# Routed experts of a two-layer gated attention and mixture-of-experts kernel: gate and up weights become the stationary operand, and the turning of the activations is dropped

## What is computed

```
# layer 0: 32 experts of inner width 128, 8 chosen for each token
h = silu(flat @ wg.T) * (flat @ wu.T)
acc = acc + w[:, None] * (h @ wd.T)
...
# layer 1: 8 experts of inner width 256, 2 chosen for each token
h = silu(xt @ w1[e].T) * (xt @ w3[e].T)
y = y + gate_e[:, None] * (h @ w2[e].T)
```

## Time and profile before

| | |
|---|---|
| device time, three executions | 1091.81, 1091.92, 1095.67 us; median 1091.92 us |
| span of the profiled execution (first to last instruction) | 1088.8 us |
| median less span: what lies around the span | 3.1 us |
| busy share of the span: TensorE, VectorE, ScalarE, GpSimd | 84%, 64%, 41%, 50% |
| granted TensorE clock, mean over the span | 0.924 |
| routed blocks of layer 0 | about 340 to 601 us of the span |
| routed blocks of layer 1 | about 923 to 1064 us of the span |

### The profile page before, as it was taken

One profiled execution on the slowest core, in us unless ns is written; L12 is line 12 of the kernel. 1 busy time (PEld: TensorE's weight loads), 2 busy tenths in 40 slices (PEclk: granted clock), 3 DMA queues, 4 the chain that ended last, 5 costly groups with the idle time before them and its releaser, 6 DMA issues.

```text
span 1088.8 us, 20608 instructions
## 1 busy us (share of the span) xinstructions
PE 911.9 (84%) x5524; PEld 711.6 (65%) x5525; DVE 701.8 (64%) x1978; ACT 441.5 (41%) x1031; POOL 546.5 (50%) x581
## 2 busy tenths in 40 slices
PE   3368888887658999999999907889999997998883
PEld 3367777777546888888888504655656564786672
DVE  5669999997796865555555268675857256443334
ACT  4558888893053444434444202022223223232220
POOL 7246655644005755555552677878600001787641
PEclk9769999998668999999999968979999997999997
DMA  8960000003103776676777874343300020466648
GB/s 247 223 122 2 1 0 0 0 2 108 44 1 87 233 221 209 217 221 208 217 185 130 291 238 133 97 141 101 107 1 20 1 77 19 84 110 136 135 67 246
DMA packets 75225, 127.44 MB, mean 117 GB/s; under 512 B 12480, under 2 KB 52032, under 8 KB 75008
## 3 DMA queue, kind: packets, MB, share of 16 engines
q0 software_dynamic: 21264, 48.02, 19.4%
q1 hardware_dynamic: 32240, 57.47, 17.4%
q10 hardware_dynamic: 21632, 20.85, 5.5%
HBM read 80.62 MB, written 36.77 MB: 108 GB/s over the span
## 4 chain that ended last, share of the span: by engine, by line
PE 54%; DVE 21%; DMA 8%; issue 7%; POOL 6%; ACT 2%; SPq 2%; DVEq 0%; ACTq 0%; POOLq 0%
PE bank L917 17%; PE bank L932 9%; PE bank L1622 5%; POOL yg L1199 4%; DVE ptl L621 4%; PE bank L906 4%; DMA sw<-in_w 4%; PE bank L427 2%; PE bank L1522 2%; DVE nmax L613 2%; PE bank L925 2%; DVE hot_hi L1341 2%; PE bank L1557 2%; PE bank L1681 2%; PE bank L1582 2%
## 5 line engine op out<-in xcount | busy, mean ns | idle before, releaser
L1182 POOL DMA_INDIRECT xg<-token_rows,gather_idx x198 | 191.7, 968 | 209.1 <-PE bank L906 86.4
L917 PE MATMUL bank<-sw,xgt 128*128 x948 | 244.9, 381 | 0.4 <-issue 0.4
L917 PEld LDWEIGHTS bank<-sw,xgt 128*128 128x128 f32 x948 | 165.4, 191 | 15.5 <-issue 0.8
L1199 POOL DMA_INDIRECT yg<-slot_rows,slot_of x128 | 142.1, 1110 | 59.9 <-issue 34.7
L1011 ACT ACTIVATE ssil<-bank 128x128 f32<-128x128 f32 x237 | 65.8, 278 | 210.8 <-PE bank L917 210.8
L932 PE MATMUL bank<-sw,sht 128*128 x474 | 145.2, 389 | 0.1
L1103 DVE COPY xgt<-bank 128x256 f32<-128x256 f32 x198 | 83.9, 424 | 85.7 <-PE bank L906 77.2
L1116 DVE COPY sht<-bank 128x128 f32<-128x128 f32 x237 | 69.2, 292 | 107.1 <-PE bank L925 106.6
L549 ACT ACTIVATE prob<-bank,nmax 128x256 f32<-128x256 f32 x256 | 111.7, 511 | 7.1 <-DVE nmax L613 7.1
L427 PE MATMUL bank<-consts,prob 128*128 128x128 f32 x512 | 84.0, 289 | 34.0 <-DVE ptl L621 31.5
L613 DVE TENSOR_REDUCE nmax<-bank 128x2 f32<-128x512 f32 x128 | 87.7, 686 | 17.3 <-PE bank L414 16.8
(11 more groups left out here) (225 smaller groups left out, 1632.2 us busy)
## 6 DMA issues: line engine op xcount, KB each, us to landing
slot_rows<-ysb ACTq DMA_DIRECT2D x79, 256.0 KB, 3.5
sw<-in_w SPq DMA_DIRECT2D x48, 384.0 KB
kst<-khl SPq DMA_DIRECT2D x32, 224.0 KB, 5.3
token_sums<-zeros SPq DMA_DIRECT2D x2, 2176.0 KB, 13.3
token_rows<-xn SPq DMA_DIRECT2D x8, 512.0 KB, 4.2
sums<-token_sums SPq DMA_DIRECT2D x8, 512.0 KB, 7.6
xg<-token_rows,gather_idx POOLq DMA_INDIRECT x198, 3.6
x<-in_x SPq DMA_DIRECT2D x4, 512.0 KB, 6.0
```

The lines of the kernel that those rows point to most:

```text
L917: mm = pe.matmul(bank[2 + k % 2][:, 0:2 * FF], xgt[:, i % 3, c * P:(c + 1) * P], w[:, :, c, :], start=(c == 0), stop=(c == CH - 1))
L1182: nc.gpsimd.indirect_dma_start(xg[:, (first + i) % XG_RING, 0:ROW[L]], None, rows[L], bass.IndirectOffsetOnAxis(gather_idx[:, i:i + 1], 0) ...
L1199: nc.gpsimd.indirect_dma_start(yg[:, t % Y_TILES, j, :], None, ybuf[L], bass.IndirectOffsetOnAxis(slot_of[:, t, j:j + 1], 0)).then_inc(s_y ...
```

## The change

The gate and up products swap their operands: the 128x128 weight pieces become the stationary operand, and the 128 turned token rows stream. A unit then has four products of 128 columns in place of two of 256, and the result comes out with the inner width on its partitions, which is what the down product wants. `hidden_transposed` on TensorE and `hidden_copied` on VectorE go, with the buffer `shid`. `hidden` writes `sht` directly.

The weights are first copied by VectorE from their slot in `sw` to one of four buffers `wgu` at fixed addresses (`gate_up_weights_copied`, 128x512 per unit, two units ahead). VectorE reads both `needed` and `wslot` for each block and waits for the weights, in both layers; TensorE no longer reads `needed` and no longer waits for a load. `ssil`, `sht`, `wgu` and the PSUM banks of the gate and up products go round four units in place of two.

```
+GU_RING = 4
...
-        ssil = sb("ssil", [P, 2, P], F32, rt)
-        shid = sb("shid", [P, 2, P], F32, rt)
-        sht = sb("sht", [P, 2, P], F32, rt)
+        ssil = sb("ssil", [P, GU_RING, P], F32, rt)
+        sht = sb("sht", [P, GU_RING, P], F32, rt)
+        wgu = sb("wgu", [P, GU_RING, 2, CH, FF], F32, rt)
...
             def gate_up(k):
                 i, u = k // halves, k % halves
                 pe.wait_ge(s_xtl, first + i + 1)
-                if k >= 2:
-                    pe.wait_ge(s_sh, UNITS + first + k - 1)
-                for c in range(CH):
-                    w = sw[:, bass.ds(slot[i] + u, 1), 0:2 * CH * FF].rearrange("p a (h c f) -> p (a h) c f", h=2, c=CH)
-                    mm = pe.matmul(bank[2 + k % 2][:, 0:2 * FF], xgt[:, i % 3, c * P:(c + 1) * P], w[:, :, c, :],
-                                   start=(c == 0), stop=(c == CH - 1))
+                pe.wait_ge(s_wgu, first + k + 1)
+                if k >= GU_RING:
+                    pe.wait_ge(s_sh, UNITS + first + k - GU_RING + 1)
+                for h in range(2):
+                    for c in range(CH):
+                        mm = pe.matmul(bank[2 + k % GU_RING][:, h * P:(h + 1) * P], wgu[:, k % GU_RING, h, c, :],
+                                       xgt[:, i % 3, c * P:(c + 1) * P], start=(c == 0), stop=(c == CH - 1))
                 mm.then_inc(s_sgate, 1)
-
-            def hidden_transposed(k):
-                pe.wait_ge(s_sh, UNITS + first + k + 1)
-                if k >= 2:
-                    pe.wait_ge(s_hte, UNITS + first + k - 1)
-                pe.transpose(bank[4 + k % 2][:, 0:P], shid[:, k % 2, :], ident).then_inc(s_ht, 1)
 
             def down(k):
                 i, u = k // halves, k % halves
-                pe.wait_ge(s_hte, UNITS + first + k + 1)
+                pe.wait_ge(s_sh, UNITS + first + k + 1)
                 if u == 0 and i >= 2:
                     pe.wait_ge(s_sye, first + i - 1)
-                pe.matmul(bank[6 + i % 2][:, 0:DIM], sht[:, k % 2, :], sw[:, bass.ds(slot[i] + u, 1), 2 * CH * FF:WCOLS],
+                pe.matmul(bank[6 + i % 2][:, 0:DIM], sht[:, k % GU_RING, :], sw[:, bass.ds(slot[i] + u, 1), 2 * CH * FF:WCOLS],
                           start=(u == 0), stop=(u == halves - 1)).then_inc(s_sy, 1)
...
-            loads = {}
 
             def block_numbers(i):
                 slot[i] = pe.value_load(wslot[0:1, i:i + 1], min_val=0, max_val=W_RING - halves)
-                if L == 1:
-                    loads[i] = pe.value_load(needed[0:1, i:i + 1], min_val=16, max_val=16 * (E0 + 2 * E1))
...
             for k in range(blocks * halves):
                 i = k // halves
                 if k % halves == 0:
-                    if L == 1:
-                        pe.wait_ge(s_sw, loads[i])
                     if i + 2 < blocks:
                         slots_transposed(i + 2)
                 gate_up(k)
                 if k % halves == 0 and i + 1 < blocks:
                     block_numbers(i + 1)
-                if k >= 1:
-                    hidden_transposed(k - 1)
                 if k >= 2:
                     down(k - 2)
-            hidden_transposed(blocks * halves - 1)
             down(blocks * halves - 2)
             down(blocks * halves - 1)
...
             def silu(k):
                 act.wait_ge(s_sgate, UNITS + first + k + 1)
-                if k >= 2:
-                    act.wait_ge(s_sh, UNITS + first + k - 1)
-                nc.scalar.activation(ssil[:, k % 2, :], bank[2 + k % 2][:, 0:FF], ACT.Silu).then_inc(s_ssil, 1)
+                if k >= GU_RING:
+                    act.wait_ge(s_sh, UNITS + first + k - GU_RING + 1)
+                nc.scalar.activation(ssil[:, k % GU_RING, :], bank[2 + k % GU_RING][:, 0:P], ACT.Silu).then_inc(s_ssil, 1)
...
         def sparse_vector(dve, L, m):
             first, blocks, halves = FIRST[L], BLOCKS[L], 1 + L
 
+            slot = {}
+
+            def gate_up_weights_copied(k):
+
+                i, u = k // halves, k % halves
+                if u == 0:
+                    loaded = dve.value_load(needed[0:1, i:i + 1], min_val=16, max_val=16 * (E0 + 2 * E1))
+                    slot[i] = dve.value_load(wslot[0:1, i:i + 1], min_val=0, max_val=W_RING - halves)
+                    dve.wait_ge(s_sw, loaded)
+                if k >= GU_RING:
+                    dve.wait_ge(s_sgate, UNITS + first + k - GU_RING + 1)
+                nc.vector.tensor_copy(wgu[:, k % GU_RING].rearrange("p h c f -> p (h c f)"),
+                                      sw[:, bass.ds(slot[i] + u, 1), 0:2 * CH * FF].rearrange("p a w -> p (a w)")).then_inc(s_wgu, 1)
+
             def slots_copied(i):
-                if L == 0:
-                    dve.wait_ge(s_sw, dve.value_load(needed[0:1, i:i + 1], min_val=16, max_val=16 * E0))
                 dve.wait_ge(s_xt, 2 * TILES + first + i + 1)
                 if i >= 3:
                     dve.wait_ge(s_sgate, UNITS + first + halves * (i - 2))
@@ -1104,32 +1105,27 @@
 
             def hidden(k):
                 dve.wait_ge(s_ssil, UNITS + first + k + 1)
-                if k >= 2:
-                    dve.wait_ge(s_ht, UNITS + first + k - 1)
-                nc.vector.tensor_tensor(shid[:, k % 2, :], ssil[:, k % 2, :], bank[2 + k % 2][:, FF:2 * FF],
+                if k >= GU_RING:
+                    dve.wait_ge(s_sy, UNITS + first + k - GU_RING + 1)
+                nc.vector.tensor_tensor(sht[:, k % GU_RING, :], ssil[:, k % GU_RING, :], bank[2 + k % GU_RING][:, P:2 * P],
                                         ALU.mult).then_inc(s_sh, 1)
-
-            def hidden_copied(k):
-                dve.wait_ge(s_ht, UNITS + first + k + 1)
-                if k >= 2:
-                    dve.wait_ge(s_sy, UNITS + first + k - 1)
-                nc.vector.tensor_copy(sht[:, k % 2, :], bank[4 + k % 2][:, 0:P]).then_inc(s_hte, 1)
 
             dve.wait_ge(m.exp, m.n["exp"] + 1)
             slots_copied(0)
+            gate_up_weights_copied(0)
             slots_copied(1)
+            gate_up_weights_copied(1)
             for k in range(blocks * halves):
                 i = k // halves
                 if k % halves == 0 and i + 2 < blocks:
                     slots_copied(i + 2)
-                if k:
-                    hidden_copied(k - 1)
+                if k + 2 < blocks * halves:
+                    gate_up_weights_copied(k + 2)
                 hidden(k)
                 if L == 0 and 0 <= i - 4 < 3 * TILES // 2:
                     if i == 4:
                         dve.wait_ge(m.cw, 1)
                     gates_of_slots(dve, i - 4)
-            hidden_copied(blocks * halves - 1)
```

More of the change, by code:

```diff
@@ L337, in gated_xattn_moe_kernel @@
         s_xtl = sem("slots_copied")
+        s_wgu = sem("gate_up_weights_copied")
         s_sye = sem("s_y_scaled")
```

## The result

The changed kernel takes 1116.7 us against 1091.9 us of the kernel before on the same chip: a ratio of 1.023, 95% interval 1.019 to 1.028. The profiled execution has a span of 1115.5 us, 26.7 more than before. The forecast was 1098.4 us: the direction and the wide range hold, the size of the loss does not (+24.8 us in place of +6.5). The forecast's own range, 1090 to 1112 us, and its 1.66 to 1.80 us for a unit of layer 0 are missed.

What follows compares the result with a forecast made beforehand. TensorE was taken to set the pace in both layers, except in a chain of loads late in layer 1. Layer 0 +14 and layer 1 -7.5 gave +6.5, so 1098.4 us; range 1076 to 1120, own range 1090 to 1112.

Steps and rivals of the forecast that it cites:

- The queue as the bound of layer 0: Layer 0, VectorE's queue: two register loads and issue steps take 1.71 us per unit, above TensorE's 1.56.
- The steps that I added up to 1.70: VectorE's queue, layer 0: copy to load 0.025, loads 0.65 and 0.72, address 0.10, two issues 0.10 each.
- 0.01 for them: VectorE's queue, layer 0: allowance in us per unit for slow loads (298 to 636 ns) that medians leave out.
- Rival 3: VectorE's register loads get slower, both at 442 ns: 1.99 us per unit of layer 0, 1142 us in all; chance 0.08.
- 1.56 forecast: TensorE's time per unit in us: turning rows 0.22, eight gate and up weight loads at 0.112 0.90, down 0.44.
- Rival 2: Layer 0: the queue runs loads beside other issues, unit under 1.56 us, TensorE stays the bound; 1075 us; chance 0.12.
- rival 1: Layer 0: VectorE's queue and TensorE near even, 1.56 to 1.66 us per unit; 1084 us at 1.62; chance 0.20.
- Rival 4: VectorE's weight copy holds up GpSimd's gathers for 0.43 us each; layer 1 ends at +0.6, 1106.5 us; chance 0.10.
- A block of 2.90: Layer 1, first stretch: a block goes from 3.19 to 2.90 us, -4.9 us over about 17 blocks.
- The terms for the rounds (-1.5): Layer 1, five rounds: work from landing to next load takes 3.9 us in place of 4.2, -0.3 each.
- the tail behind them (-1.7): Layer 1, six blocks after the last round: shorter blocks save 1.7 us.
- The 3.1 us added to the span: Whole kernel: time around the profiled span of 1088.8 us, added to the forecast span of 1095.3.

Runs made afterwards that it cites:

- third load: The changed kernel with a third register load per block on VectorE's queue, of a value that nothing uses: 1213.4 us.
- short copy: The changed kernel with both loads, copying only 16 of 512 gate and up weight columns from the fifth unit of a layer on: 1111.1 us.
- later store: The changed kernel with both loads, ScalarE's store in layer 0 issued after the next block's copy of the sums, about 0.5 us later: 1110.2 us.

## Why the size was off

**The queue as the bound of layer 0: right.** One load less gave TensorE its 1.546 us (the median), one more cost 0.60 per unit, and a copy of 16 columns changed nothing. The steps that I added up to 1.70 measured 1.66 (the sum of the medians between starts on the queue).

**The term that failed** is "0.01 for them", for the loads that medians leave out. It was (445 - 305) + (316 - 305) = 151 ns, so 1.66 + 0.15 = 1.81, near the 1.83 measured; over 158 units that makes +33 us in place of +12.5. I took the tail from a kernel in which 10 of 159 loads were over 400 ns, but there the one load sat at 0.25 to 0.5 or at 1.75 to 2.0 us after a store's issue (all but a handful of the 156 in steady state). In the changed kernel the second load, 0.7 us after the first, met the harmful time in about two of five units. The row gave a price that held for its moments alone. Rival 3 had the direction, slower loads, and its sign, loads over 0.4 us, came true for the second load (0.445 in the mean). But it took both loads at 0.44, 1.99 us per unit, and charged that to a load behind another; the third load, with the first of three slow and the last never, shows that this isn't the cause.

**TensorE: right.** Gate records start 0.112 us apart, a unit without the queue's bound takes 1.546 (1.56 forecast). Rival 2's time of 1075 us is thus what the change gives with one load (1073.4), though not by rival 2's mechanism; rival 1 asked for a queue of 1.56 to 1.66.

**Rival 4, the copy locking GpSimd out: not seen.** Gathers of layer 0 have a mean of 970 ns against 959 before; in the kernel with one load 143 of 156 run beside a copy, and their mean is 962. The short copy left the unit as it was. What the Trainium skill's page SBUF — State Buffer (section SBUF: two separate sides) says of fp32 copies holding up GpSimd's descriptors would have shown in these; at one copy of 0.43 us per unit, no run here shows it.

**Layer 1.** A block of 2.90: measured 2.87, and the first 19 blocks gained 6.2 us. The terms for the rounds (-1.5) and the tail behind them (-1.7) failed: the last 19 blocks got 1.5 us longer. I used rates at full clock for the two units after a landing, 2.68 us, and in the round shown they took 4.56. The work after a landing did get shorter, by 0.4 to 0.6 us where the clock stayed (4.6 to 4.2 and 4.0); where it fell, the round got 1.0 to 1.2 us longer than before. TensorE also stood still for longer, 13.9 of the last 73.8 us in place of 9.4 of 72.3: the shorter blocks left it without work while the loads took no less time. That a fall costs this much is shown round by round, in kernels whose layer 1 has the same code; why it comes in some rounds and not in others is open.

**The time around the span.** The 3.1 us added to the span set the median of other executions against the profiled one. In each later run the time and the span of one execution differ by 1.8 to 2.0 us (1117.3 and 1115.5 for the changed kernel). The forecast of the median, 1091.9 + 6.5, doesn't hang on it.

## What to carry to other kernels

A register load costs its engine's queue 0.6 us or more here, and two per loop step can become the bound while every engine has idle time: count what the queue issues, not only what the engine computes, and work a second number out of the first by register arithmetic. Price a repeated wait by the mean of its records and ask at which moments of the step they were taken; a median of 305 hid a mean of 445. Where a stage waits for loads anyway, faster compute may give nothing back: it lengthens TensorE's idle wait, and the work behind it may run at the lower clock.

## What was unexpected of the hardware

- A VectorE register load takes 300 ns or about 600: in the changed kernel 60 of the 69 that start 0.75 to 1.25 us after the issue of a 256 KB store by ScalarE are over 400 ns (the 12 at 1.0 to 1.25 us have a mean of 631), and none of the 140 that start 2.0 to 3.5 us after it. What in the store does it isn't shown, and loads are slow in layer 1 too, without such a store. The page DMA: Bandwidth & Descriptors of the Trainium skill (section Latency and other measured facts) puts a floor of about 600 ns under such a load; that is what a disturbed one takes here, and most take half.
- Behind a wait of TensorE of 2.6 us the granted clock was 0.79 and then 0.57, and two units took 4.56 us in place of 2.64. The wait's length alone doesn't tell: the clock stayed at 1.00 behind 3.2 us in the short copy and fell behind 1.4 us in the later store.
- An address with a division and a remainder is still one instruction on the queue: 180 ns in place of 64, cheaper than the load that it replaces.
